# A fused audio tower on one core: the order of steps rewritten in two halves of two chunks, with top-2 per half

## Chip, core and metric

The kernel runs on one core of a Trainium2 chip. Its engines work side by side and each in its own program order: TensorE (PE, with its weight loads PEld), VectorE (DVE), ScalarE (ACT), GpSimd (POOL) and SyncE (SP), which here only issues DMAs. They wait for one another by semaphores. The metric is the device time of one execution in microseconds (us), lower is better; the median of the runs is compared.

## The reference

The input is 64 sequences of 375 steps with 16 features. Everything is float32. Five blocks follow one another, each but the first a residual on the layer norm of what is there:

```python
y = jnp.einsum('bpi,di->bpd', patches, W) + b          # 45 patches per sequence, D = 64
...
scores = jnp.einsum('bhqd,bhkd->bhqk', q, k) / jnp.sqrt(jnp.float32(HD)).astype(q.dtype)
attn = jax.nn.softmax(scores.astype(jnp.float32), axis=-1).astype(q.dtype)
...
probs = jax.nn.softmax(logits, axis=-1)
top2_vals, top2_idx = jax.lax.top_k(probs, 2)          # over 8 experts
h = jax.nn.gelu(xf @ w1 + bb1, approximate=False)      # every expert for every token
y = h @ w2 + bb2
...
S = S * dec_t[:, None, :] + sa[:, :, None] * b_t[:, None, :] + v_t[:, :, None] * k_t[:, None, :]
o_t = jnp.einsum('bvk,bk->bv', S, r_t)                 # a scan over the 45 tokens
...
ye = h @ Wr[l, e].T + br[l, e]                         # 2 layers, one of 16 experts per sequence
h = jax.nn.relu(shared + routed + h)
```

The kernel does the scan in closed form: it builds small triangular matrices per sequence, inverts them in levels, and multiplies.

## The kernel before

The 64 sequences are 32 pairs (two sequences lie on the two halves of the 128 partitions), and the pairs are `C` = 4 chunks of `PP` = 8 pairs. A chunk's activations are a tile of 128 x 360 floats (`W` = 8 x 45). All state of a chunk lies in its part of `arena`, and each chunk owns two of the eight PSUM banks (`PS`), so chunks are independent of each other; only the weights and the top-2 step are shared. Within a chunk nearly every step waits for the step ahead of it, because it uses the same two banks.

`schedule()` (L82) writes one list of steps `(name, i, c)`: a name, an index within it and a chunk. Each engine's program is made by walking that list and emitting its part of each step, so the list is the program order of all five engines. In the old list a stage runs over all four chunks before the next one starts; TensorE has three other chunks to work on while one waits for VectorE or ScalarE. The stages, by the names in the code:

- `tok`, two norms (`mean`, `var`), `q`, `k`, `v`: up to 49 us. They are the same after the change.
- attention: for each of 8 pairs and each chunk the scores `s` (TensorE, then maximum L611 and subtraction L613 on VectorE), exponential `e` (ScalarE L394), transposes `t` (TensorE L849, copy on ScalarE L397), weighted sum `pv` (TensorE, then reciprocal L621 and multiply L623 on VectorE). `LAG` = 2 is the distance between `t` and `pv` in units.
- `attT`, `wo`, norm 2, `gate`, then `top2`: one chain of 17 dependent steps on VectorE (L655 to L672) over all chunks' gate logits, with one exponential on ScalarE (L405), and a copy per chunk (L677). Then `cwT`, `cw2`, `b2` (the expert weights transposed and split in three bf16 parts).
- 8 experts: `hid` (TensorE, gelu on ScalarE L415) and `y` (TensorE, copy on ScalarE L419, multiply on VectorE L694, addition on GpSimd L313). `hid` of the next expert waits for the multiply of this one in the same chunk.
- norm 3 with `mixes`: its `var` step carries on VectorE the norm's product (L571), the difference of neighbours (L584, L585) and four mixes (L588); then `rk`, `vw`.
- the projections `aw`, `ab`, `gh`, `gg`, `kk`, `bon`, `kb`; `m`, `vt` and the inverse `lx`, `lt` in four levels; the solve `u`, `y2`, `z`, `w`, `o`; norm `gn`, `ro`, norm 5, `f`.
- the routed layers `r` (two layers, each 64 small matmuls of 32 columns per chunk against weights that SyncE gathered by DMA), `fo` and the output DMA.

ScalarE holds one set of function tables at a time. `tables(name)` (L350) emits a table load where the next function needs another set than the one loaded: exponential and logarithm are in one set, gelu and sigmoid/tanh each in another. SyncE's list: constants and input, 64 weight DMAs for routed layer 0, then 64 for layer 1, of which a chunk's 16 wait for that chunk's `h1` (attention added).

## Time and profile before

| | us |
|---|---|
| median of 3 runs | 394.02 |
| lowest, highest | 389.51, 397.53 |
| the profiled execution | 395.19 |
| its span on the core | 393.2 |
| TensorE busy in it | 326.8 (83%) |
| VectorE, ScalarE, GpSimd busy | 220.6, 197.7, 142.3 |

The profile is of one execution. The busy time of an engine is the sum of its instructions; what is left of the span it waits or has nothing to do. A matmul in float32 shows as two records, each with its weight load. The granted clock (PEclk) is given as a share of TensorE's full 2.4 GHz; the other level is 0.50, 1.2 GHz.

### The profile page before, as it was taken

What the parts mean: (1) busy time and instruction counts of PE and PEld (TensorE: products, weight loads), DVE (VectorE), ACT (ScalarE), POOL (GpSimd) and SP (SyncE); (2) the same over time, 40 slices, a digit from 0 to 9 for tenths busy, and PEclk for the clock granted to TensorE, in tenths of its full rate; (3) what the DMA queues carried; (4) which work ended last, traced back from release to release, by engine and by line L of the source; (5) the groups of instructions that cost most, each with busy time, mean ns of one, the idle gap of its engine ahead of it and who ended that gap; (6) DMA issues with size and microseconds to landing.
All of it is one profiled execution on the core that took longest, in us unless ns stands there. A gap on an engine that the chain in (4) does not pass through costs nothing.

```text
span 393.2 us, 13416 instructions
## 1 busy us (share of the span) xinstructions
PE 326.8 (83%) x5712; PEld 222.4 (57%) x5712; DVE 220.6 (56%) x446; ACT 197.7 (50%) x382; POOL 142.3 (36%) x146
## 2 busy tenths in 40 slices
PE   4999999999995999999677984597777799798465
PEld 2447876766862734343233544597776699345342
DVE  4567687787368632333595889965665303751002
ACT  1665465445454367677747794356000774646120
POOL 9009999512000055564243006699900000310000
PEclk9999999999997799999959998699999999879996
DMA  8622222110012221221000000000000000000002
GB/s 274 262 59 62 65 58 65 51 49 3 3 47 61 58 58 56 60 63 33 1 0 0 2 0 0 3 4 3 3 6 5 3 5 3 0 0 5 3 5 77
DMA packets 20563, 14.92 MB, mean 38 GB/s; under 512 B 2328, under 2 KB 19352, under 8 KB 20376
## 3 DMA queue, kind: packets, MB, share of 16 engines
q1 hardware_dynamic: 20504, 14.07, 11.5%
q8 instruction: 45, 0.74, 0.7%
q14 instruction: 14, 0.11, 0.1%
HBM read 13.32 MB, written 0.74 MB: 36 GB/s over the span
## 4 chain that ended last, share of the span: by engine, by line
PE 52%; DVE 17%; issue 12%; ACT 10%; POOL 8%; POOLq 0%; DVEq 0%
PE PS L785 48%; POOL arena L313 7%; PE PS L849 4%; DVE arena L588 2%; DVE arena L732 2%; DVE arena L571 2%; ACT arena L373 2%; ACT arena L370 1%; ACT arena L476 1%; ACT arena L485 1%; DVE PS L520 1%; ACT arena L489 1%; ACT arena L365 1%; DVE arena L735 1%; DVE arena L584 1%
## 5 line engine op out<-in xcount | busy, mean ns | idle before, releaser
L785 PE MATMUL PS<-arena,K 128*128 128x360 f32 (+2 forms) x576 | 149.7, 515 | 21.2 <-DVE arena L588 7.3
L785 PE MATMUL PS<-arena 128*45 128x45 f32 (+6 forms) x3648 | 118.5, 221 | 31.7 <-issue 15.4
L785 PEld LDWEIGHTS PS<-arena 128*45 128x45 f32 (+4 forms) x3648 | 100.7, 127 | 50.6 <-issue 36.4
L785 PEld LDWEIGHTS PS<-arena,K 128*128 128x128 f32 (+2 forms) x576 | 71.0, 183 | 81.8 <-issue 22.6
L313 POOL TENSOR_TENSOR arena<-arena 128x360 f32<-128x360 f32 x32 | 30.0, 948 | 68.8 <-DVE arena L694 68.2
L694 DVE TENSOR_TENSOR arena<-PS,arena 128x360 f32<-128x360 f32 x32 | 17.0, 533 | 33.7 <-ACT arena L419 33.7
L785 PE MATMUL PS<-K,arena 128*45 128x32 f32 (+4 forms) x768 | 26.1, 223 | 4.8 <-DVE arena L677 4.2
L785 PEld LDWEIGHTS PS<-K,arena 128*45 128x45 f32 (+2 forms) x768 | 25.3, 132 | 6.9 <-DVE arena L677 4.9
L397 ACT COPY arena<-PS 128x360 f32<-128x360 f32 x32 | 14.8, 467 | 24.5 <-PE PS L849 24.4
L415 ACT ACTIVATE arena<-PS,K 128x720 f32<-128x720 f32 x32 | 24.9, 861 | 2.5 <-PE PS L785 2.5
L341 POOL TENSOR_TENSOR arena<-arena 128x360 f32<-128x360 f32 x4 | 4.4, 1112 | 56.4 <-DVE arena L579 56.4
L302 POOL TENSOR_TENSOR arena<-arena,K 128x360 f32<-128x360 f32 x32 | 24.1, 799 | 0.0
L419 ACT COPY arena<-PS 128x360 f32<-128x360 f32 x32 | 14.8, 462 | 14.8 <-PE PS L785 14.8
L485 ACT ACTIVATE arena<-arena,K 128x360 f32<-128x360 f32 x8 | 4.3, 591 | 35.5 <-DVE arena L767 35.5
L849 PE MATMUL PS<-K,arena 128*128 128x128 f32 x128 | 20.8, 285 | 0.7 <-DVE arena L623 0.7
L571 DVE TENSOR_TENSOR arena<-arena 128x360 f32<-128x360 f32 x24 | 12.7, 531 | 14.8 <-ACT arena L373 14.8
L611 DVE TENSOR_REDUCE smax<-PS 128x8 f32<-128x360 f32 x32 | 16.9, 529 | 7.1 <-PE PS L785 7.0
L778 DVE SCALAR_TENSOR_TENSOR arena<-PS,K,arena 128x360 f32<-128x360 f32 x4 | 2.4, 593 | 32.5 <-PE PS L785 32.5
L365 ACT ACTIVATE arena<-arena 128x360 f32<-128x360 f32 x24 | 11.8, 503 | 17.1 <-DVE arena L565 15.7
L290 POOL TENSOR_TENSOR WG<-WG,K 128x2048 f32<-128x2048 f32 x4 | 15.2, 3816 | 13.2 <-DMA WG<-wr 13.2
L565 DVE TENSOR_TENSOR arena<-arena,PS 128x360 f32<-128x360 f32 x24 | 12.3, 528 | 10.4 <-PE PS L785 9.3
L394 ACT ACTIVATE arena<-arena 128x360 f32<-128x360 f32 x32 | 16.4, 513 | 3.3 <-DVE arena L613 3.3
(126 smaller groups left out, 420.2 us busy)
## 6 DMA issues: line engine op xcount, KB each, us to landing
WG<-wr SPq DMA_DIRECT2D x64, 64.0 KB, 1.9
arena<-wr SPq DMA_DIRECT2D x64, 64.0 KB, 1.8
arena<-xT SPq DMA_DIRECT2D x4, 368.0 KB, 4.8
K<-consts SPq DMA_DIRECT2D x1, 1171.0 KB, 10.7
K<-consts SPq DMA_DIRECT2D x1, 852.0 KB, 10.4
out<-arena SPq DMA_DIRECT2D x4, 180.0 KB, 1.9
K<-consts SPq DMA_DIRECT2D x1, 510.0 KB, 8.3
K<-consts SPq DMA_DIRECT2D x1, 352.0 KB, 9.1
```

Of the source, the lines that this page charges most:

```text
L290: g.tensor_tensor(w, w, shared, ALU.add).then_inc(sem["wsum"], 1)
L302: g.tensor_tensor(a(c, KX_ + i * W).rearrange("q (h t) -> q h t", t=T), a(c, slot(4) + i * T, T).unsqueeze(1).broadcast_to([128, NH, T]), ...
L313: g.tensor_tensor(a(c, H_), a(c, H_), a(c, slot(3 + i % 2)), ALU.add).then_inc(sem["acc"], 1)
L365: s.activation(a(c, sq), a(c, xc), ACT.Square).then_inc(sem["ln_sq"], 1)
L394: s.activation(pb, pb, ACT.Exp).then_inc(sem["s_exp"], 1)
L397: s.copy(a(c, PT_, 512).rearrange("q (r t) -> q r t", t=64)[:, :, 0:T], bank(c, 1, 512).rearrange("q (r t) -> q r t", t=64)[:, :, 0:T]).th ...
L415: s.activation(halves(a(c, slot(6), 2 * W)), both(c), ACT.Gelu, bias=k("b1", i, i + 1)).then_inc(sem["gelu"], 1)
L571: v.tensor_tensor(a(c, dst), a(c, xc), a(c, sq), ALU.mult).then_inc(sem["ln_out"], 1)
L611: v.tensor_reduce(smax[:, c, :], sc, AX.X, ALU.max).then_inc(sem["s_max"], 1)
L694: v.tensor_tensor(a(c, slot(3 + i % 2)), bank(c, 0), a(c, slot(8)), ALU.mult).then_inc(sem["y_mul"], 1)
L785: return nc.tensor.matmul(o, l, r, start=start, stop=stop)
L849: last = nc.tensor.transpose(bank(c, 1, 128, 128 * g), a(c, PB_ + 128 * g, 128), k("identf"))
```

## The change

The four chunks become two halves, a (chunks 0 and 1) and b (2 and 3). Up to the first scores everything stays. From attention on the new `schedule()` writes each block for one half, and `ahead(x, y)` merges two of them: it takes x step by step and puts in steps of y evenly between. So the list becomes: attention of a alone; attention of b with the after-attention steps of a; experts of a with the after-attention steps of b; experts of b with the mixes of a; mixes of b with projections of a; inverse of a with projections of b; inverse of b with solve and finish of a; solve of b alone; finish of b with the routed layers of a; routed layers of b. A step that is given as a list (norm 2's and norm 3's `var`, the first `hid`) is put in for both chunks of the half together. In attention the distance from `t` to `pv` is one unit where it was two. Top-2 runs once per half, over half of the elements, with its semaphore counts offset; the bias splitting moves from unit (4, 0) to (2, 0). Waits that counted steps in the old order now name chunk or step. No instruction of TensorE, GpSimd or SyncE is added or removed; VectorE has top-2's chain twice at half the size (the copies per chunk stay four in all), and ScalarE has 18 table loads where it had 5, and one exponential more.

```diff
+TOP2_STEPS = 17
...
+    halves_of_chunks = [range(0, C // 2), range(C // 2, C)]
+    def stage(cs, *steps):
+        return [(name, i, c) for name, i in steps for c in cs]
+    def norm(cs, k):
+        return stage(cs, ("mean", k), ("var", k))
+    def ahead(x, y):
+        out, taken = [], 0
+        for n, step in enumerate(x):
+            out.append(step)
+            while taken < len(y) and (taken + 1) * len(x) <= (n + 1) * len(y):
+                group = y[taken]
+                out += group if isinstance(group, list) else [group]
+                taken += 1
+        return out
+    def attention(cs):
+        out = []
+        units = [(i, c) for i in range(PP) for c in cs]
+        for n in range(len(units) + 1):
+            if n < len(units):
+                i, c = units[n]
+                out.append(("t", i, c))
+            if n:
+                out.append(("pv",) + units[n - 1])
+            if n < len(units) and i < PP - 1:
+                out.append(("s", i + 1, c))
+            if n:
+                i, c = units[n - 1]
+                if i < PP - 1:
+                    out.append(("e", i + 1, c))
+        return out
+    def after_attention(cs):
+        return (stage(cs, ("attT", 0), ("wo", 0)) + stage(cs, ("mean", 2)) + [stage(cs, ("var", 2))]
+                + stage(cs, ("gate", 0)) + [("top2", 0, cs[0])]
+                + [stage(cs, ("hid", 0))] + stage(cs, ("cwT", 0), ("cw2", 0), ("b2", 0)))
+    def experts(cs):
+        out = stage(cs, ("y", 0))
+        for i in range(1, E):
+            out += stage(cs, ("hid", i), ("y", i))
+        return out
+    def mix(cs):
+        out = stage(cs, ("mean", 3)) + [stage(cs, ("var", 3))]
+        for c in cs:
+            out += [("mixes", 0, c), ("rk", 0, c)]
+        return out + stage(cs, ("vw", 0))
+    def project(cs):
+        return stage(cs, ("aw", 0), ("ab", 0), ("gh", 0), ("gg", 0), ("kk", 0), ("bon", 0), ("kb", 0))
+    def invert(cs):
+        out = stage(cs, ("m", 0), ("m", 1), ("vt", 0))
+        for i in range(len(LEVELS)):
+            out += stage(cs, ("lx", i), ("lt", i))
+        return out
+    def solve(cs):
+        return stage(cs, ("u", 0), ("y2", 0), ("z", 0), ("w", 0), ("o", 0))
+    def finish(cs):
+        return norm(cs, 4) + stage(cs, ("ro", 0)) + norm(cs, 5) + stage(cs, ("f", 0))
+    def routed(cs):
+        return stage(cs, ("r", 0), ("r", 1), ("fo", 0))
+    a, b = halves_of_chunks
+    both_halves = range(C)
+    order = stage(both_halves, ("tok", 0)) + norm(both_halves, 0) + norm(both_halves, 1)
+    order += stage(both_halves, ("q", 0), ("k", 0), ("v", 0), ("s", 0), ("e", 0))
+    order += attention(a)
+    order += ahead(attention(b), after_attention(a))
+    order += ahead(experts(a), after_attention(b))
+    order += ahead(experts(b), mix(a))
+    order += ahead(mix(b), project(a))
+    order += ahead(invert(a), project(b))
+    order += ahead(invert(b), solve(a) + finish(a))
+    order += solve(b)
+    order += ahead(finish(b), routed(a))
+    order += routed(b)
+    flat = []
+    for step in order:
+        flat += step if isinstance(step, list) else [step]
+    return flat
...
-        def gate(r, n=C * PP * E):
-
-            return a(0, slot(14) + C * PP * E * r, n)
+        def gate(c, r, n=C // 2 * PP * E):
+
+            return a(c, slot(14) + C // 2 * PP * E * r, n)
...
                 elif name == "top2":
                     tables(LN_EXP)
                     act.wait_ge(sem["g_sub"], n)
-                    s.activation(gate(0), gate(0), ACT.Exp).then_inc(sem["g_exp"], 1)
+                    s.activation(gate(c, 0), gate(c, 0), ACT.Exp).then_inc(sem["g_exp"], 1)
...
-                    if (i, c) == (PP // 2, 0):
+                    if (i, c) == (2, 0):
                         split_biases()
...
                 elif name == "top2":
                     dve.wait_ge(sem["cst2"], 16)
-                    dve.wait_ge(sem["gate_mm"], C)
-                    steps = [0]
+                    dve.wait_ge(sem["gate_mm"], c + C // 2)
+                    steps = [TOP2_STEPS * (n - 1)]
+                    rows_here = C // 2 * PP
...
-                    step(v.tensor_tensor(chunks(gate(0)), logits,
-                                         k("gb").unsqueeze(1).unsqueeze(1).broadcast_to([128, C, PP, E]), ALU.add))
+                    step(v.tensor_tensor(chunks(gate(c, 0)), logits,
+                                         k("gb").unsqueeze(1).unsqueeze(1).broadcast_to([128, C // 2, PP, E]), ALU.add))
                     step(v.tensor_reduce(top, prob, AX.X, ALU.max))
                     v.tensor_tensor(prob, prob, wide(top), ALU.subtract).then_inc(sem["g_sub"], 1)
-                    dve.wait_ge(sem["g_exp"], 1)
+                    dve.wait_ge(sem["g_exp"], n)
...
-                    for cc in range(C):
+                    for cc in range(C // 2):
                         def thrice(r):
-                            return gate(r)[:, cc * small:(cc + 1) * small].rearrange(
+                            return gate(c, r)[:, cc * small:(cc + 1) * small].rearrange(
                                 "q (p e) -> q p e", e=E).unsqueeze(2).broadcast_to([128, PP, 3, E])
-                        v.tensor_tensor(a(cc, CW_, 3 * small).rearrange("q (p r e) -> q p r e", r=3, e=E), thrice(1),
+                        v.tensor_tensor(a(c + cc, CW_, 3 * small).rearrange("q (p r e) -> q p r e", r=3, e=E), thrice(1),
                                         thrice(0), ALU.mult).then_inc(sem["cw"], 1)
...
                 elif name == "hid":
                     if i == 0:
-                        pe.wait_ge(sem["g_steps"], 1)
+                        pe.wait_ge(sem["g_steps"], TOP2_STEPS * (c // (C // 2)) + 1)
                     else:
                         pe.wait_ge(sem["y_mul"], COUNT["y", i - 1, c])
...
                 elif name == "y":
                     if i == 0:
-                        pe.wait_ge(sem["cwT"], n)
-                        pe.wait_ge(sem["b2_add"], n)
-                    pe.wait_ge(sem["gelu"], n)
+                        pe.wait_ge(sem["cwT"], c + 1)
+                        pe.wait_ge(sem["b2_add"], c + 1)
+                    pe.wait_ge(sem["gelu"], COUNT["hid", i, c])
```

How the lists of instructions move, at three places. Rows are instructions in program order, with a count where several alike follow; the line numbers of the new kernel are 37 or 38 higher.

VectorE, around the first top-2 (its chain begins at L655 before, at L693 now). Before, all of attention is done, and the norm of four chunks stands ahead of it:

```order
L621 RECIPROCAL orec<-PS 128x8
L623 TENSOR_TENSOR arena<-PS,orec 128x64
L629 TENSOR_TENSOR arena<-arena,PS 128x360 x4
L565 TENSOR_TENSOR arena<-arena,PS 128x360 x4
L571 TENSOR_TENSOR arena<-arena 128x360 x4
L655 TENSOR_TENSOR arena<-PS,K 128x256
L657 TENSOR_REDUCE arena<-arena 128x32
L658 TENSOR_TENSOR arena<-arena 128x256
L660 TENSOR_REDUCE arena<-arena 128x32
L661 RECIPROCAL arena<-arena 128x32
```

After: softmax and weighted sum of the second half's attention (L648, L650, L658, L660) stand ahead of and behind it.

```order
L648 TENSOR_REDUCE smax<-PS 128x8
L650 TENSOR_TENSOR arena<-PS,smax 128x8x45
L658 RECIPROCAL orec<-PS 128x8
L660 TENSOR_TENSOR arena<-PS,orec 128x64
L693 TENSOR_TENSOR arena<-PS,K 128x128
L695 TENSOR_REDUCE arena<-arena 128x16
...
L706 TENSOR_TENSOR arena<-arena 128x128
L710 TENSOR_TENSOR arena<-arena 128x128
L715 TENSOR_TENSOR arena<-arena 128x192 x2
L648 TENSOR_REDUCE smax<-PS 128x8
L650 TENSOR_TENSOR arena<-PS,smax 128x8x45
L658 RECIPROCAL orec<-PS 128x8
```

The chain has moved from a place between two stages to the middle of attention, and acts on 128 elements where it acted on 256.

VectorE, in the experts and the mixes behind them (L694, now L732, is an expert's multiply; L588, now L625, the mixes). Before:

```order
L689 TENSOR_TENSOR arena<-arena,PS 128x360 x4
L694 TENSOR_TENSOR arena<-PS,arena 128x360 x32
L565 TENSOR_TENSOR arena<-arena,PS 128x360 x4
L571 TENSOR_TENSOR arena<-arena 128x360
L584 TENSOR_TENSOR arena<-arena 128x8x44
L585 TENSOR_SCALAR arena<-arena 128x8
L588 SCALAR_TENSOR_TENSOR arena<-arena,K 128x360 x4
L571 TENSOR_TENSOR arena<-arena 128x360
L584 TENSOR_TENSOR arena<-arena 128x8x44
```

After, in the second half's experts:

```order
L602 TENSOR_TENSOR arena<-arena,PS 128x360
L732 TENSOR_TENSOR arena<-PS,arena 128x360 x2
L608 TENSOR_TENSOR arena<-arena 128x360
L621 TENSOR_TENSOR arena<-arena 128x8x44
L622 TENSOR_SCALAR arena<-arena 128x8
L625 SCALAR_TENSOR_TENSOR arena<-arena,K 128x360 x4
L608 TENSOR_TENSOR arena<-arena 128x360
L621 TENSOR_TENSOR arena<-arena 128x8x44
L622 TENSOR_SCALAR arena<-arena 128x8
L625 SCALAR_TENSOR_TENSOR arena<-arena,K 128x360 x4
L732 TENSOR_TENSOR arena<-PS,arena 128x360 x3
L738 TENSOR_SCALAR arena<-arena,K 128x360
```

The first half's mixes now stand between two multiplies of the second half's experts.

TensorE, towards the end (32x45 are the small matmuls of the routed layers, 128x360 x2 from two arena tiles the steps of the last norms). Before, the last norms and the first layer:

```order
L785 MATMUL PS<-arena 64x45 x128
L785 MATMUL PS<-arena,K 128x360 x28
L785 MATMUL PS<-oneh,rb_split 128x360 x2
L785 MATMUL PS<-arena,WG 32x45 x64
L785 MATMUL PS<-oneh,rb_split 128x360 x2
L785 MATMUL PS<-arena,WG 32x45 x64
```

After, from the second half's first mean on:

```order
L823 MATMUL PS<-arena,K 128x360 x2
L823 MATMUL PS<-oneh,rb_split 128x360 x2
L823 MATMUL PS<-arena,WG 32x45 x64
L823 MATMUL PS<-arena,K 128x360 x2
L823 MATMUL PS<-oneh,rb_split 128x360 x2
L823 MATMUL PS<-arena,WG 32x45 x64
L823 MATMUL PS<-arena,K 128x360 x2
L823 MATMUL PS<-oneh,rb_split 128x360 x2
L823 MATMUL PS<-arena 32x45 x64
L823 MATMUL PS<-arena,K 128x360 x2
L823 MATMUL PS<-oneh,rb_split 128x360 x2
L823 MATMUL PS<-arena 32x45 x64
```

Norm steps of the second half now stand between the routed passes of the first, where eight passes followed one another.

## Rows read from the trace of the kernel before

**Rows 1.** The page, busy time, share and instructions of each engine.

```profile
PE 326.8 (83%) x5712; PEld 222.4 (57%) x5712; DVE 220.6 (56%) x446; ACT 197.7 (50%) x382; POOL 142.3 (36%) x146
```

**Rows 2.** Windows: start:end, length, each engine's busy time (instructions), PEclk, DMA.

```profile
49.00:102.20 53.20, 52.50 (x676) 36.92 (x675) 42.57 (x122) 27.01 (x62) 28.54 (x23) 1.00 0.15 42
102.20:136.50 34.30, 28.11 (x482) 21.09 (x481) 21.10 (x50) 16.33 (x31) 0.00 (x0) 0.85 0.16 47
136.50:189.60 53.10, 52.95 (x279) 20.65 (x279) 19.29 (x38) 36.33 (x62) 29.98 (x32) 1.00 0.18 51
189.60:215.00 25.40, 15.87 (x39) 7.98 (x39) 17.61 (x34) 16.98 (x32) 6.95 (x7) 0.80 0.00 0
215.00:252.10 37.10, 26.60 (x220) 18.04 (x220) 33.01 (x52) 22.98 (x45) 13.17 (x14) 0.92 0.00 1
252.10:303.90 51.80, 41.08 (x1594) 39.92 (x1596) 31.53 (x43) 13.88 (x30) 30.50 (x29) 0.96 0.02 4
303.90:333.80 29.90, 26.36 (x960) 25.96 (x954) 8.98 (x15) 18.98 (x35) 0.00 (x0) 1.00 0.02 4
333.80:356.40 22.60, 19.18 (x57) 9.55 (x56) 14.24 (x24) 13.07 (x27) 4.45 (x4) 0.85 0.00 1
356.40:386.00 29.60, 17.70 (x1046) 13.56 (x1044) 0.00 (x0) 7.44 (x11) 0.00 (x0) 0.94 0.01 4
...
386.00:393.20 7.20, 4.25 (x16) 1.48 (x16) 2.37 (x4) 0.75 (x1) 0.00 (x0) 0.74 0.28 105
```

**Rows 3.** Timeline in attention: start, length, engine, line, what [idle before].

```profile
59.58 0.53 DVE L611 TENSOR_REDUCE smax<-PS 128x8 f32<-128x360 f32 x1 [0.33 <-PE PS L785]
...
60.97 0.51 ACT L394 ACTIVATE arena<-arena 128x360 f32<-128x360 f32 x1
...
61.37 0.53 DVE L611 TENSOR_REDUCE smax<-PS 128x8 f32<-128x360 f32 x1 [0.32 <-PE PS L785]
```

**Rows 4.** Instructions grouped by line and shape: busy us, mean ns, idle.

```profile
L694 DVE TENSOR_TENSOR arena<-PS,arena 128x360 f32<-128x360 f32 x32 | 17.0, 533 | 33.7 <-ACT arena L419 33.7
...
L419 ACT COPY arena<-PS 128x360 f32<-128x360 f32 x32 | 14.8, 462 | 14.8 <-PE PS L785 14.8
...
L550 DVE SCALAR_TENSOR_TENSOR K<-rb_split,K 51x256 f32<-51x256 bf16 x1 | 0.5, 476 | 0.0
```

**Rows 5.** Timeline in top-2: VectorE's first and last rows, ScalarE's switch.

```profile
118.79 0.43 DVE L655 TENSOR_TENSOR arena<-PS,K 128x256 f32<-128x256 f32 x1 [1.02 <-PE PS L785]
...
127.40 1.16 DVE L677 TENSOR_TENSOR arena<-arena 128x192 f32<-128x192 f32 x4
...
120.59 1.28 ACT L352 ACT_TABLE_LOAD   x1
121.89 3.11 ACT L415 ACTIVATE arena<-PS,K 128x720 f32<-128x720 f32 x4
```

**Rows 6.** Timeline of TensorE in the first experts.

```profile
138.53 0.83 PE L785 MATMUL PS<-arena,K 128*64 128x360 f32 x4
...
139.55 0.83 PE L785 MATMUL PS<-arena,K 128*64 128x360 f32 x4
...
140.56 3.45 PE L785 MATMUL PS<-arena,K 64*128 64x360 f32 x20
```

**Rows 7.** Timeline of VectorE in norm 3, one chunk's start to the next.

```profile
197.21 0.53 DVE L571 TENSOR_TENSOR arena<-arena 128x360 f32<-128x360 f32 x1
...
201.83 0.52 DVE L571 TENSOR_TENSOR arena<-arena 128x360 f32<-128x360 f32 x1
```

**Rows 8.** Timeline of TensorE in the first routed layer.

```profile
362.60 1.35 PE L785 MATMUL PS<-arena,WG 128*32 128x45 f32 x111
365.99 0.39 PE L785 MATMUL PS<-arena,WG 128*32 128x45 f32 x17 [2.04 <-issue]
```

**Rows 9.** Windows around top-2, columns as in group 2.

```profile
124.00:126.00 2.00, 0.00 (x0) 0.00 (x0) 1.85 (x5) 1.00 (x2) 0.00 (x0) 1.00 0.22 66
128.00:130.00 2.00, 2.00 (x60) 2.00 (x58) 0.81 (x4) 0.46 (x1) 0.00 (x0) 0.50 0.22 64
```

64 lines of the change are left out of this document (8 added, 56 removed).

## The prediction

> **What bounds the kernel now.** I read the busy times first: TensorE is busy for 326.8 of 393.2 us, so all that an order can win is its idle 66 us [rows 1]. Next the busy times by stage, to see where that idle time lies [rows 2]. In attention and in the eight experts TensorE is full: 52.50 of 53.20 us and 52.95 of 53.10. The holes are elsewhere: 6.2 us between attention and experts (34.30 less 28.11), 9.5 in the token mixes, 10.5 in the projections, 10.7 in the triangular inverse, 3.5 in the solve, 3.4 in norms and output projection, 14.9 in the routed layers with the tail (17.70 busy of 29.60, then 4.25 of 7.20). They have three causes. First, one engine works while TensorE waits: top-2 holds VectorE from 118.79 to 128.56 [rows 5]; in the projections VectorE is busy 33.01 of 37.10 us [rows 2]. Second, TensorE runs 111 short matmuls in 1.35 us and then nothing until 365.99, which the trace puts down to issue, not to a wait [rows 8]. Third, the clock: in 124 to 126 TensorE did nothing, and in 128 to 130 it runs at 0.50 of full speed, the lower level of 1.2 GHz [rows 9].
>
> **The parts, costed.** The 66 us can be filled only where two halves overlap, and each half now has two chunks in flight instead of four. I went through the new order engine by engine: a step starts when its engine has done the step ahead of it and its inputs are there. The first 49 us don't change. Each stretch below is set against half of the old stages in it [rows 2].
>
> (1) Attention of the first half, alone. The old pace is one unit per 1.79 us (59.58 to 61.37). From the end of a score matmul, two VectorE operations (0.53 each) and the exponential (0.51) must end before that chunk's transposes, some 1.7 us with hand-overs [rows 3]. The new order puts transposes, weighted sum and scores of the other chunk in between, 1.8 us of TensorE. So it just fits, and 16 units take 28.8. The four bias-splitting operations, at most 0.48 each [rows 4], now lie in a loop without slack, +1.5. Total 30.5, against 26.6: **+3.9**.
>
> (2) Attention of the second half with the after-attention steps of the first. TensorE has 26.3 us of attention and half of 28.11 at mean clock 0.85, 12: 38.3. The second top-2 cost is new: top-2 took 9.8 us for four chunks (118.79 to 128.56) [rows 5]. With half the elements its 17 steps save only some 0.13 us each (an estimate: 0.42 at 256 elements and 0.53 at 360 make 1 ns per element) and two of four copies go, so 7.0 us remain, per half; bounds are 9.3 (no operation gets shorter) and 4.9 (everything halves), 2 us either way in (2) and in (3). Behind it in VectorE's queue stands the softmax of the next unit; TensorE has 3.8 us left that needs none of it and idles some 5.4. The grouped variance steps hold ScalarE for four operations, 2 us more. Rest 1: 46.7 against 26.6 + 17.2 = 43.8: **+2.9**.
>
> (3) Experts of the first half with the after-attention steps of the second. An output takes 1.01 us of TensorE (138.53 to 139.55), a hidden layer (3.45 - 0.83) / 4 = 0.65 [rows 6]; four of each make the 6.64 us that an expert takes now. With four chunks the chain hidden, gelu (0.78), output, copy (0.46), multiply (0.53) [rows 4 to 6] hides behind the other three; with two it takes some 3.75 us against 3.3 us of matmuls, which the inserted steps fill. 16 outputs and 14 hidden layers are 25.3 us; 25.3 + 12 = 37.3, and 4.5 of stalls, mostly top-2 again with two table loads at 1.28 [rows 5]: 41.8 against 43.8: **-2.0**.
>
> (4) Experts of the second half with the mixes of the first. TensorE: 25.3 and half of 15.87 at clock 0.80, with its last matmuls some 7: 32.3. But the variance group carries all mixing: 4.6 us per chunk on VectorE (197.21 to 201.83) [rows 7], two chunks in a row, behind a table load, a logarithm and an exponential. The experts' next multiply waits behind that; TensorE has one round, 3.3 us, to run meanwhile: 8 us lost. Four more table loads sit between two gelus or behind them, 4 us. Total 44.3 against 26.6 + 12.7 = 39.3: **+5.0**.
>
> (5) Mixes of the second half with projections of the first: VectorE has (17.61 + 33.01) / 2 = 25.3 us [rows 2]; with waits for table loads 29, against 31.3: **-2.3**. (6) Inverse of the first half with projections of the second: VectorE again, (31.53 + 33.01) / 2 = 32.3 plus the last level's 3, and 6 of waits, since a chunk's 4 us of scaling steps stand ahead of the inverse's subtractions: 41.6 against 18.5 + 25.9 = 44.4: **-2.8**. (7) Inverse of the second half with solve and norms of the first: TensorE (41.08 x 0.96 + 26.36 + 19.18 x 0.85) / 2 = 41, start stall 4.5, rest 1: 46.7 against 25.9 + 15.0 + 11.3 = 52.2: **-5.5**. (8) Solve of the second half alone: 15.1 against 15.0: **0**. (9) Norms of the second half with the routed layers of the first: the routed layers' issue gaps (11.9 us idle in eight passes) and the norms' waits cover each other: 19 against 11.3 + 14.8 = 26.1: **-7.1**. (10) Routed layers of the second half and the tail: 20.6 against 14.8 + 7.2 = 22.0, the tail having two outputs to write instead of four: **-1.4**. No DMA moves into the way: the 64 layer-1 weight loads start when a chunk's attention has been added, earlier for the first half, and are needed only in (6).
>
> Sum: +3.9 + 2.9 - 2.0 + 5.0 - 2.3 - 2.8 - 5.5 - 7.1 - 1.4 = -9.3, with all matmuls behind the new holes at full clock. They won't be: five holes of 3 us and more (one in 2, one in 3, two in 4, one at the start of 7, one in 8) can each be followed by some 5 us at 0.50, as in [rows 9], which costs 2.5 where TensorE is what is waited for: 0 to 13 us, less what before loses so and after wins back. I take +6, the middle. That is -3.3 on the profiled execution of 395.2: 391.9. The median of the runs is 394.0, which would make 390.7. **391 us.**
>
> A page speaks against the change. The new order needs 18 table loads where the old has 5. In the trace a load takes 1.28 us and the gelu starts at 121.89, 0.02 after it [rows 5], so the 13 added loads cost at most 16.7 us. The Trainium skill (ScalarE: Activation LUTs, What ACT_TABLE_LOAD costs) says that each switch takes 1283 ns and about 1380 ns of drain on top. By that rule the 13 loads would cost 34.6 us, and the sum, which exposes about a third of them, would be some 6 us higher; the trace agrees with the first figure and shows no drain.
>
> **The rivals.** *The holes fill* (0.30): ScalarE and VectorE waits overlap better than my walk has it, the clock stays up. For it: 66 us idle against the 9 that I win. Then the -9.3 stands, or twice that: 376 to 386. *Table loads decide* (0.12; slower): every added load lands between a matmul and the gelu, tanh or logarithm that TensorE waits for, in (3) to (5). Against it: many are issued while ScalarE waits anyway. By the page's rule above this rival would cost 17.9 us more; the trace is against that part. My sum has about 6 of the 16.7 exposed; all make +11: 402. It ends slower once more than about 11 of the 13 are exposed. *Attention does not fit* (0.11; slower): the slack of 0.1 us per unit in (1) isn't there. Each of 32 units longer by 0.35 gives +11, 402. It decides from 0.33 us per unit. Against it: the steps in [rows 3] add up to just under the pace. *The order does nothing* (in my case): gains at the end equal losses in the middle, 395.
>
> **How the numbers follow.** My forecast has 0.47: 384 to 399. A measurement of this kernel tells about 2% from no change, 386 to 402. Faster: nearly all of the first rival and the low edge of mine, 0.34. Slower: most of the two slow rivals and a little of mine, 0.20. Within 2%: 0.46. The range leaves out the best fifth of the fast rival and the worst of the slow ones: 377 to 404.
>
> **What would show it.** Attention of the first half at 1.8 us per unit, ending near 80 us. Two top-2 blocks of about 7 us on VectorE, each with a TensorE hole of 3 to 5. A hole of about 8 us in TensorE within the second half's experts. The routed layers of the first half without issue gaps of 1.5 to 2 us. TensorE's mean clock below 0.94. I'm wrong if attention runs at over 2 us per unit, if the table loads follow straight on waits of TensorE throughout, or if the span to the start of the second half's routed layers is far from 369 (the stretches up to there, with the clock's 6).

## The result and the profile after

The changed kernel takes 427.65 us, the median of 4 runs (424.81 to 429.6); the kernel before, measured beside it, 393.91 us (389.51 to 397.53). The ratio is 1.089, with a 95% interval of 1.077 to 1.101: slower by 9%, outside the predicted range of 377 to 404. The profiled execution has a span of 422.7 us and a mean granted clock of 0.922; the kernel before had 393.2 us and 0.943.

The page of the changed kernel, busy times, answers to [rows 1]:

```profile
PE 343.2 (81%) x5712; PEld 220.7 (52%) x5712; DVE 242.5 (57%) x464; ACT 218.5 (52%) x396; POOL 143.1 (34%) x146
```

TensorE has the same 5712 matmuls. Its idle time has grown from 66.4 to 79.5 us and its busy time from 326.8 to 343.2. Two questions: where is the new idle time, and how can the same matmuls be busy for longer?

The busy times by window, cut where the prediction's ten stretches begin and end, answer to [rows 2] (columns as there):

```profile
49.00:94.00 45.00, 28.62 (x356) 19.01 (x354) 35.89 (x64) 15.20 (x32) 27.70 (x22) 0.81 0.18 51
94.00:144.50 50.50, 43.14 (x588) 28.93 (x586) 32.65 (x94) 23.34 (x47) 0.00 (x0) 0.93 0.15 44
144.50:188.20 43.70, 39.33 (x354) 16.96 (x356) 20.07 (x48) 32.02 (x50) 14.40 (x15) 1.00 0.16 45
188.20:236.80 48.60, 40.21 (x163) 14.98 (x163) 17.43 (x36) 33.70 (x53) 19.62 (x21) 0.90 0.02 5
236.80:269.20 32.40, 21.10 (x97) 11.52 (x97) 25.85 (x43) 23.39 (x41) 9.32 (x10) 0.87 0.00 1
269.20:318.20 49.00, 39.36 (x1009) 32.04 (x1007) 38.94 (x52) 21.97 (x43) 21.96 (x21) 0.88 0.01 3
318.20:368.20 50.00, 47.41 (x1398) 39.86 (x1394) 29.40 (x43) 22.88 (x46) 18.38 (x17) 0.99 0.01 4
368.20:383.20 15.00, 12.06 (x323) 11.47 (x324) 2.26 (x4) 7.65 (x14) 0.00 (x0) 0.89 0.01 2
383.20:403.20 20.00, 16.14 (x547) 9.39 (x545) 7.00 (x13) 9.18 (x17) 2.11 (x2) 1.00 0.02 4
403.20:422.70 19.50, 13.59 (x536) 8.93 (x536) 2.26 (x4) 4.79 (x6) 0.00 (x0) 0.80 0.12 41
```

The first stretch stands out: 45.0 us, of which TensorE works 28.62, while VectorE is "busy" 35.89. What TensorE waited for, over the whole kernel (total us, times, longest), puts it in one row, the first:

```profile
PE PS L887 <- ACT arena L431: 21.4, 5, 14.1
...
PE PS L823 <- issue: 5.2, 6, 1.6
```

The transposes (L887) waited 14.1 us in one piece for an exponential (L431), which waited for VectorE's subtraction. VectorE's timeline there, and GpSimd's:

```profile
59.35 9.87 DVE L585 CAST rb_split<-K 51x256 bf16<-51x256 f32 x1
69.25 0.48 DVE L587 SCALAR_TENSOR_TENSOR K<-rb_split,K 51x256 f32<-51x256 bf16 x1
69.76 3.79 DVE L590 CAST rb_split<-K 51x256 bf16<-51x256 f32 x1
73.58 0.48 DVE L592 SCALAR_TENSOR_TENSOR rb_split<-rb_split,K 51x256 bf16<-51x256 bf16 x1
...
55.49 5.31 POOL L339 TENSOR_TENSOR arena<-arena,K 128x360 f32<-128x360 f32 x7
60.76 0.78 POOL L318 TENSOR_TENSOR K<-K 128x128 f32<-128x128 f32 x2
61.49 7.58 POOL L327 TENSOR_TENSOR WG<-WG,K 128x2048 f32<-128x2048 f32 x2
69.58 3.82 POOL L327 TENSOR_TENSOR WG<-WG,K 128x2048 f32<-128x2048 f32 x1 [0.51 <-DMA WG<-wr]
```

These are the four operations of the bias splitting, which the change moved from unit (4, 0) to unit (2, 0). A cast of 51x256 elements takes 9.87 us, and the second 3.79. In the kernel before, the same two took 0.28 and 0.29 us, at 82.55:

```profile
82.55 0.28 DVE L548 CAST rb_split<-K 51x256 bf16<-51x256 f32 x1
...
83.37 0.29 DVE L553 CAST rb_split<-K 51x256 bf16<-51x256 f32 x1
...
62.37 11.36 POOL L290 TENSOR_TENSOR WG<-WG,K 128x2048 f32<-128x2048 f32 x3
86.88 3.81 POOL L290 TENSOR_TENSOR WG<-WG,K 128x2048 f32<-128x2048 f32 x1 [13.15 <-DMA WG<-wr]
```

The long casts end when GpSimd stops: the first at 69.22, in the 0.51 us in which GpSimd waits for a DMA (61.49 + 7.58 = 69.07 to 69.58), the second at 73.55, behind the last addition (73.40). Each ends about 0.15 us behind that. In the old order the splitting fell into GpSimd's wait of 13.15 us. That is a reading so far; the experiments test it.

### The profile page after: what moved, and what is told of

Same layout as the page of the kernel before. It is cut to its first block, busy times and chain, and to the rows that moved or that the text cites. A ratio compares the mean times of both kernels' runs of the same rounds, so it can differ in the third digit from the quotient of the medians.

```text
span 422.7 us, 13449 instructions
## 1 busy us (share of the span) xinstructions
PE 343.2 (81%) x5712; PEld 220.7 (52%) x5712; DVE 242.5 (57%) x464; ACT 218.5 (52%) x396; POOL 143.1 (34%) x146
## 4 chain that ended last, share of the span: by engine, by line
PE 52%; DVE 23%; ACT 16%; issue 5%; POOL 2%; POOLq 0%; DVEq 0%
PE PS L823 49%; PE PS L887 3%; DVE rb_split L585 2%; ACT L389 2%; DVE arena L625 2%; ACT arena L407 2%; DVE arena L608 2%; ACT arena L410 2%; DVE arena L650 1%; ACT arena L452 1%; DVE smax L648 1%; DVE arena L732 1%; ACT arena L513 1%; ACT arena L402 1%; ACT arena L456 1%
## 5 line engine op out<-in xcount | busy, mean ns | idle before, releaser
L823 PE MATMUL PS<-arena,K 128*128 128x360 f32 (+2 forms) x576 | 157.4, 515 | 27.8 <-ACT arena L452 7.8
L823 PE MATMUL PS<-arena 128*45 128x45 f32 (+6 forms) x3648 | 131.2, 227 | 23.7 <-ACT arena L502 10.8
L823 PEld LDWEIGHTS PS<-arena 128*45 128x45 f32 (+4 forms) x3648 | 108.3, 132 | 46.0 <-issue 36.0
L823 PEld LDWEIGHTS PS<-arena,K 128*128 128x128 f32 (+2 forms) x576 | 64.7, 178 | 84.3 <-issue 22.0
L887 PE MATMUL PS<-K,arena 128*128 128x128 f32 x128 | 21.5, 293 | 22.0 <-ACT arena L431 21.4
L732 DVE TENSOR_TENSOR arena<-PS,arena 128x360 f32<-128x360 f32 x32 | 16.8, 532 | 36.5 <-ACT arena L456 36.5
L887 PEld LDWEIGHTS PS<-K,arena 128*128 128x128 f32 x128 | 14.8, 147 | 34.9 <-ACT arena L431 32.3
L452 ACT ACTIVATE arena<-PS,K 128x720 f32<-128x720 f32 x32 | 26.6, 860 | 7.2 <-PE PS L823 7.1
L823 PEld LDWEIGHTS PS<-K,arena 128*45 128x45 f32 (+2 forms) x768 | 24.4, 125 | 7.5 <-issue 4.2
L431 ACT ACTIVATE arena<-arena 128x360 f32<-128x360 f32 x32 | 16.4, 514 | 19.2 <-DVE arena L650 19.0
L648 DVE TENSOR_REDUCE smax<-PS 128x8 f32<-128x360 f32 x32 | 16.9, 529 | 12.9 <-PE PS L823 12.9
L456 ACT COPY arena<-PS 128x360 f32<-128x360 f32 x32 | 14.5, 460 | 14.4 <-PE PS L823 14.1
L327 POOL TENSOR_TENSOR WG<-WG,K 128x2048 f32<-128x2048 f32 x4 | 15.2, 3813 | 14.5 <-DMA WG<-wr 14.5
```

Source lines behind the costliest of these rows:

```text
L431: s.activation(pb, pb, ACT.Exp).then_inc(sem["s_exp"], 1)
L452: s.activation(halves(a(c, slot(6), 2 * W)), both(c), ACT.Gelu, bias=k("b1", i, i + 1)).then_inc(sem["gelu"], 1)
L456: s.copy(a(c, slot(8)), bank(c, 1)).then_inc(sem["cwb"], 1)
L648: v.tensor_reduce(smax[:, c, :], sc, AX.X, ALU.max).then_inc(sem["s_max"], 1)
L732: v.tensor_tensor(a(c, slot(3 + i % 2)), bank(c, 0), a(c, slot(8)), ALU.mult).then_inc(sem["y_mul"], 1)
L823: return nc.tensor.matmul(o, l, r, start=start, stop=stop)
```

## The experiments

Theory P: the casts wait for GpSimd, and that is the main cause. Rival Q: the new attention loop (two chunks, a distance of one unit) is slow by itself. Behind that comes what is left over. All ratios are to the kernel before, measured on the same chip in the same session. The runs fall into four sessions on different chips, in which the kernel before took 389.9 to 395.4 us, so two runs of different sessions are compared by their ratios and not by their times.

**1. The splitting at another place in the changed kernel.**

```diff
-                    if (i, c) == (2, 0):
+                    if (i, c) == (6, 1):
                         split_biases()
```

> The changed kernel with one edit: the bias splitting moves from unit (2, 0) of attention to unit (6, 1), at about 76 us, where GpSimd has ended its layer-0 additions and waits for a DMA until 87 us. Theory P (the two casts of the splitting, 9.87 and 3.79 us in the changed kernel's trace where they took 0.28 in the old one, wait for GpSimd's additions of weights, which run at 61.5 to 73.4 us): each cast is back at about 0.3 us, TensorE's hole of 14.13 us at 75.7 goes but for 1 to 1.5 us, and the kernel takes 12.5 to 14 us less than the changed one, so a ratio to the kernel before of 1.053 to 1.057. Rival Q (the new attention loop with a distance of one unit is what is slow, and the casts only show a wait that the loop has anyway): the hole moves to the new place or is spread over the units, and the time stays within 3 us of the changed kernel, ratio 1.08 to 1.09.

407.48 us against 395.41; ratio 1.026 (1.017 to 1.036), where 1.053 to 1.057 was expected. The profile (span 405.8) has both casts at their usual length, and the first stretch takes 29.8 us instead of 45.0:

```profile
L590 DVE CAST rb_split<-K 51x256 bf16<-51x256 f32 x1 | 0.3, 285 | 0.0
L585 DVE CAST rb_split<-K 51x256 bf16<-51x256 f32 x1 | 0.3, 275 | 0.0
```

```profile
49.00:78.80 29.80, 27.37 (x360) 18.11 (x357) 23.54 (x66) 15.71 (x33) 24.65 (x22) 1.00 0.22 61
```

P holds and Q falls: the loop itself costs 29.8 us, near what was forecast. The gain is larger than expected: 15.2 us in this stretch and 16.9 between the spans (by the ratios it is more, 1.089 to 1.026). It is the hole, and a granted clock of 1.00 in this stretch where it was 0.81. Some 10 to 12 us of the loss remain.

**2. The splitting early in the kernel before.**

```diff
-                    if (i, c) == (PP // 2, 0):
+                    if (i, c) == (2, 0):
                         split_biases()
```

> The kernel before with one edit: the bias splitting moves from unit (4, 0) to unit (2, 0), at about 63 us, where GpSimd adds its layer-0 weights (62.4 to 73 us in the old trace). Theory P: the casts take together 8 to 12 us as in the changed kernel, and with four chunks in turn on TensorE the hole behind them is 7 to 12 us: ratio 1.02 to 1.03. Rival Q (the order of the halves is the cause): ratio 1.00, both casts about 0.3 us. Between them lies: the casts are long but the other chunks hide most of it, ratio 1.01.

400.67 us, 5.3 more than before, ratio 1.010 (1.002 to 1.019): little as a time, but the trace is plain. One move of four short operations, nothing else, and a hole appears in a stage that had none:

```profile
68.33 5.76 DVE L548 CAST rb_split<-K 51x256 bf16<-51x256 f32 x1
...
62.55 11.38 POOL L290 TENSOR_TENSOR WG<-WG,K 128x2048 f32<-128x2048 f32 x3
```

```profile
PE PS L849 <- DVE arena L623: 6.0, 1, 6.0
```

The first cast ends at 74.09, 0.15 us behind the last of three additions (73.94), and the second, with GpSimd idle, takes 0.28. The hole is below the expected 7 to 12 us because here, with four chunks in turn, a unit comes round more slowly: unit (2, 0) comes at 68.33, 9 us later, so less of GpSimd's work is left to wait for.

**3. The splitting in place, GpSimd's additions later.**

```diff
             def shared_plus_identity():
 
+                pool.wait_ge(sem["h1"], 2)
                 pool.wait_ge(sem["cst4"], 16)
```

> The changed kernel with the bias splitting left at unit (2, 0), but GpSimd begins its layer-0 additions of weights only when attention has been added in chunks 0 and 1 (about 95 us in this kernel). Theory P: the casts take about 0.3 us each, the hole at 75.7 goes, and 12 to 14 us come back, less what the additions cost at their new place: they then run beside norm 2 and the first top-2, whose VectorE operations read two tiles of SBUF, so up to one addition (3.8 us) may be lost there again. Ratio 1.055 to 1.07. Rival Q: ratio 1.08 to 1.09 and long casts or a hole at the same place with GpSimd idle.

418.69 us, ratio 1.060 (1.052 to 1.068), within the expected 1.055 to 1.07: better than the changed kernel (1.089), and 11.2 us slower than run 1 in the same session. The first cast takes 1.58 us (GpSimd still runs its last products of attention), the second 0.28. The rest went where the expectation feared. The additions now run from 94.84 to 110.53 without a gap, and the norm's product (L609, two inputs in SBUF, 0.53 us as a rule) is caught in two chunks:

```profile
94.84 15.70 POOL L328 TENSOR_TENSOR WG<-WG,K 128x2048 f32<-128x2048 f32 x4
...
102.37 4.10 POOL L328 TENSOR_TENSOR WG<-WG,K 128x2048 f32<-128x2048 f32 x1
...
101.44 1.36 DVE L609 TENSOR_TENSOR arena<-arena 128x360 f32<-128x360 f32 x1 [0.63 <-ACT arena L411]
102.72 4.14 DVE L609 TENSOR_TENSOR arena<-arena 128x360 f32<-128x360 f32 x1
106.79 0.19 DVE L659 RECIPROCAL orec<-PS 128x8 f32<-128x8 f32 x1
```

These two products behave otherwise than the casts. The first addition that they meet ends at 102.41, the next at 106.47, and each product ends 0.39 us behind one of these, though the following addition has begun by then: a product waits for one addition and gets in ahead of the next. The addition that it gets ahead of is the one that pays, 4.10 us for 3.81. The cast of the changed kernel passed five such places, between operations of GpSimd that followed each other, and got in at none of them.

The operations on PSUM behind it (L659 and on) run at their usual length while the additions go on to 110.53.

**4. Another instruction in place of the cast.**

```diff
-                v.tensor_copy(hi, rb).then_inc(sem["rb_steps"], 1)
+                v.tensor_tensor(hi, rb, rb, ALU.max).then_inc(sem["rb_steps"], 1)
```

> The changed kernel with the splitting at its place, but the two casts (one input in SBUF) are written as a maximum of the tile with itself (two inputs in SBUF, bfloat16 out, the same values). Theory P1 (it is the cast as such that waits for GpSimd: only it is held among VectorE's operations): the maximum takes about 0.5 us, and 12.5 to 14 us come back, ratio 1.053 to 1.057. Theory P2 (a VectorE operation with two inputs in SBUF waits too, as the product L752 of 0.53 us that takes 4.03 us at 288.5 us beside the layer-1 additions would have it): the maximum takes 9 to 10 and 3 to 4 us as the casts do, ratio 1.08 to 1.09. The Trainium skill (SBUF — State Buffer, Who interferes with whom) is on P2's side: by it both forms contend with a GpSimd operation that reads SBUF.

The four runs took 421.01 to 431.88 us against 395.41, that is 1.065 to 1.092 of it, too wide a spread to choose between P1 (1.053 to 1.057) and P2 (1.08 to 1.09) by a ratio. The trace chooses. P2 holds in kind: this operation, which is no cast and has its two inputs in SBUF, is caught too. Its size is another than expected, one wait of 13.76 us in place of one of 9 to 10 and one of 3 to 4. It waits for everything that GpSimd has in a row, products, sums and three additions, from 60.36 to 74.12; the second maximum (74.66, 0.42 us) then meets nothing:

```profile
60.36 13.76 DVE L585 TENSOR_TENSOR rb_split<-K 51x256 bf16<-51x256 f32 x1
...
49.72 12.08 POOL L339 TENSOR_TENSOR arena<-arena,K 128x360 f32<-128x360 f32 x16
61.76 0.78 POOL L318 TENSOR_TENSOR K<-K 128x128 f32<-128x128 f32 x2
62.49 11.34 POOL L327 TENSOR_TENSOR WG<-WG,K 128x2048 f32<-128x2048 f32 x3
```

The rule stands in the Trainium skill (SBUF — State Buffer, Who interferes with whom): VectorE and GpSimd share one pair of ports as an exclusive lock, which a VectorE operation needs when it has two inputs in SBUF or is a cast or copy in a two-port mode. The runs agree on what is caught (9.87, 5.76 and 13.76 us, and 0.28 or 0.42 with GpSimd idle). The same section has the lock held for the whole instruction; how long a VectorE operation waits when GpSimd's instructions follow each other differs between the runs here, from the rest of one addition (run 3) to all that are in a row (this run).

**5. The other place with the same pattern.** In the changed kernel, and in run 1, GpSimd's layer-1 additions meet the projections of the second half. Of run 1, where L749 waits for the first addition (to 272.30), L752 for the second (to 276.17):

```profile
271.27 1.23 DVE L749 TENSOR_SCALAR arena<-arena,K,oneka 128x360 f32<-128x360 f32 x1
272.54 4.03 DVE L752 TENSOR_TENSOR arena<-arena 128x360 f32<-128x360 f32 x1
...
268.49 7.68 POOL L327 TENSOR_TENSOR arena<-arena,K 128x2048 f32<-128x2048 f32 x2
```

The edit, on top of run 1's:

```diff
-                elif name == "lx" and i == 0:
-                    add_shared(1, c)
+                elif name == "lx" and i < 2 and c >= C // 2:
+                    add_shared(1, 2 * i + c - C // 2)
```

> The order in halves with the splitting moved to unit (6, 1), and beside it GpSimd's four layer-1 additions of weights (3.85 us each) moved from the inverse of each half (a's lay beside the projections of b, at 268.5 to 276.2 us in that kernel) to the first two levels of the inverse of b. Theory P (a VectorE operation with both inputs in SBUF waits for GpSimd's addition: L752 took 4.03 us where it takes 0.53, L749 1.23 for 0.46, and TensorE had a hole of 2.6 us behind L802): these operations are back at their usual length and 3 to 5 us go against the kernel with the splitting alone moved, ratio 1.013 to 1.02. Rival Q (the hole is given back by the next wait, since VectorE and ScalarE bound this stretch): 0 to 1.5 us go, ratio 1.022 to 1.03.

404.03 us, ratio 1.029 (1.021 to 1.037), not to be told from run 1's 1.026: as a time it is the rival's 1.022 to 1.03. The mechanism is confirmed in its stretch: L752 takes 0.53 again, L749 0.46, and from the first eviction of `m` in chunk 0 to that in chunk 2 it is 44.4 us instead of 47.5. Whether those 3 us reach the end can't be resolved with these intervals. A third operation is caught in the changed kernel, in run 1 and still in this one (2.50 us here), the scaling L810 of the solve, which takes 0.49 us in the second half. Of the changed kernel:

```profile
336.01 2.49 DVE L810 TENSOR_SCALAR arena<-arena,K 128x512 f32<-128x512 f32 x1
```

**6. The table loads.** Every function that needs a set becomes sigmoid, and one load is made, in run 1's order and in the old one (in both outputs the functions are missing).

```diff
-                if loaded[0] != name:
-                    s.preload_act_table_set(name)
+                if loaded[0] is None:
+                    s.preload_act_table_set("sigmoid_and_others")
```

> The order in halves with the splitting moved (as in the run that moved it to unit (6, 1)), but every function of ScalarE that needs a set is replaced by sigmoid and one table load is made in all instead of 18: the output leaves out exponential, logarithm, gelu and tanh, the instructions and their sizes stay. To be read against the same edit of the kernel before. Theory T (the 13 added loads of 1.28 us, 16.7 us of ScalarE, are what the middle loses): the order in halves comes within 3 us of the kernel before under the same edit. Theory N (most loads fall in ScalarE's idle time or beside other holes, and the middle loses by its chains): it stays 8 to 12 us behind it, as with the loads (12.1 us between medians).

> The kernel before with every set function of ScalarE replaced by sigmoid and one table load instead of 5: the output leaves out exponential, logarithm, gelu and tanh. It is the control of the run with the halves. Four loads of 1.28 us go, of which the one in top-2 (120.59 us) and the one ahead of the first gelu lie on TensorE's path. Both theories: 1 to 5 us less than before, ratio 0.988 to 1.0.

402.40 us (1.025, 1.018 to 1.032) and 390.43 us (0.995, 0.992 to 0.998): 12.0 us apart, where run 1 and the kernel before are 12.1 apart with the loads. Theory N: 13 more loads cost the order in halves nothing that can be measured. The hole in experts b with mixes a shows it at one place: it was 3.49 us behind two loads, and stays 3.36 without them, now behind VectorE's norm and mixes for two chunks (6.5 us in a row).

**7. Top-2.** Run 1 with each half's chain cut from 17 to 9 waited steps (`TOP2_STEPS = 9`; the output leaves out the second expert).

> The order in halves with the splitting moved to unit (6, 1), and top-2's chain cut from 17 to 9 waited steps in each half (the output leaves out the second expert and the choice among equals): 8 steps of 0.325 us, 2.6 us a half. Theory S (the chain of each half lies on TensorE's path: it stands idle 3.06 us at 111.0 and 1.40 at 106.2 behind a's): 4 to 6 us less than with the splitting alone moved, half a stretch of lower clock behind it gone too, ratio 1.011 to 1.017. Rival U (only a's lies there, b's hides under the experts): 2 to 3 us less, ratio 1.018 to 1.022. Rival V (given back at the next wait): ratio 1.024 to 1.03.

405.22 us, ratio 1.036 (1.027 to 1.044): no gain to be seen, which is rival V's reading, though above its 1.024 to 1.03. TensorE's wait behind the first chain went only from 3.25 to 2.58 us.

**8. Only the end in halves.** The kernel before up to the inverse, then solve a; solve b with finish a; finish b with routed a; routed b.

```diff
+    order += solve(a)
+    order += ahead(solve(b), finish(a))
+    order += ahead(finish(b), routed(a))
+    order += routed(b)
```

> The kernel before, order unchanged through the inverse (four chunks a stage, top-2 once, bias splitting at unit (4, 0), 5 table loads); only its end is cut in halves, as the change does: solve of a, then solve of b with finish of a, finish of b with the routed layers of a, routed layers of b. The waits on the weights' sum name layer and chunk as in the change. Theory E (the change's end gains what the milestones of the changed kernel show, 6.1 us in finish b with routed a and 2.5 us in routed b with the tail, and its middle loses): 6 to 11 us less than before, ratio 0.972 to 0.985. Rival F (the end gains only because the middle left an idle ScalarE and VectorE behind, or the granted clock takes it back): ratio 0.99 to 1.005.

392.64 us, ratio 1.001 (0.996 to 1.005), over 10 and 17 runs: nothing.

**9. Halves from the inverse, and halves from norm 3.** The old order up to `kb` in the one, up to the last expert in the other, and the change's order behind.

```diff
+    order += invert(a)
+    order += ahead(invert(b), solve(a) + finish(a))
```

```diff
+    order += mix(a)
+    order += ahead(mix(b), project(a))
+    order += ahead(invert(a), project(b))
+    order += ahead(invert(b), solve(a) + finish(a))
```

> The kernel before, its order unchanged through the projections (kb); from there the halves as the change has them: inverse of a alone, inverse of b with solve and finish of a, solve of b, finish of b with the routed layers of a, routed layers of b. Theory G (the change's late stretches are good: between the first m of b and the end the order in halves took 102.3 us with the splitting moved, where half an inverse and the stages behind it take 109.5 us in the kernel before): 3 to 7 us less than before, less 1 to 3 us for the inverse of a alone with two chunks to turn over; ratio 0.98 to 0.995. Rival F (as with the solve and norms in halves, which gave nothing: what the merge hides comes back in matmul bursts that no longer follow each other and in the clock): ratio 0.995 to 1.01.

> The kernel before, its order unchanged through the experts; from norm 3 on the halves as the change has them, starting with the mixes of a alone. It splits what is left of the loss (12.1 us with the splitting moved) at the last expert. Theory M (the loss lies in the stretches ahead of it: attention b with after-attention a at 50.1 us for 43.8, experts a at 46.5 for 43.8, experts b with mixes a at 47.8 for 39.3, together 17.5 us; from mixes b on the same kernel took 181.9 us where the halves of before take 191 us): mixes of a alone take 13 to 17 us, and this kernel takes 5 us less to 2 us more than before, ratio 0.987 to 1.005. Rival R (it lies in the projections and the inverse merged with them, where TensorE waits 9.1 and 8.0 us): 6 us or more above before, ratio 1.015 or more.

From the inverse: 390.06 us against 392.42, ratio 0.994 (0.990 to 0.998), the only order tried here that beats both kernels, by 0.6%, a small gain whose interval leaves out 1. From norm 3: 392.11 us, ratio 1.001 (0.997 to 1.004), theory M. Its profile cuts the loss cleanly. Norm 3 of the second half begins (its square on ScalarE) at 206.80 in it and at 223.93 in run 1; from there to the end it is 182.0 us (span 388.8) in the one and 181.9 (405.8) in the other. So all that run 1 loses against this order, 17 us, lies ahead of that point: in attention, top-2 and the experts, with what is put in between them.

**10. The experts in halves, alone.**

```diff
+    for cs in (range(0, C // 2), range(C // 2, C)):
+        order += [("y", 0, c) for c in cs]
+        for i in range(1, E):
+            order += [("hid", i, c) for c in cs] + [("y", i, c) for c in cs]
```

> The kernel before with one edit: the experts of chunks 0 and 1 run first, then those of chunks 2 and 3, with nothing beside them; all else in the old order. Theory H (two chunks can't cover the round of hid, gelu, y, copy and multiply: two chunks have 3.34 us of TensorE work an expert, half of the 6.68 us pitch of four chunks, and a chunk's round takes about 4.6 us by its parts, 0.65 + 0.84 + 1.0 + 0.46 + 0.53 and four hand-overs of 0.2 to 0.3): TensorE waits about 1.3 us an expert, 16 times, so 15 to 22 us more than before, ratio 1.04 to 1.055. Then the experts in halves of the change live on their filling, and where the other half's steps leave a place empty or come in a bunch TensorE stands. Rival I (two chunks are enough, the round is covered): ratio 0.995 to 1.01.

400.81 us against 389.86, ratio 1.028 (1.019 to 1.036). Theory H has the sign, not the size: 11 us instead of 15 to 22. TensorE's timeline of one expert:

```profile
149.93 2.66 PE L787 MATMUL PS<-arena,K 64*128 64x360 f32 x12
152.52 0.33 PE L787 MATMUL PS<-arena,KB 128*128 128x360 bf16 x1
152.78 0.83 PE L787 MATMUL PS<-arena,K 128*64 128x360 f32 x4
153.54 0.33 PE L787 MATMUL PS<-arena,KB 128*128 128x360 bf16 x1
153.97 2.66 PE L787 MATMUL PS<-arena,K 64*128 64x360 f32 x12
```

One expert of two chunks takes 153.97 - 149.93 = 4.04 us; in the old order, with four, 6.68 (the copy L419 of chunk 0 stands at 151.16 and 157.84), so 3.34 for two. That is 0.70 us a pass, 10 us over 14 passes. Little of it shows as idle. The list of waits has none here, and the window of six passes, 24.23 us, has TensorE busy for 22.79:

```profile
140.77:165.00 24.23, 22.79 (x110) 7.15 (x112) 6.39 (x12) 15.85 (x24) 11.36 (x12) 1.00 0.21 61
```

So 0.24 us of a pass are idle, in gaps too short for the list, and 0.46 are counted as busy. 20 such records take 3.45 us in [rows 6], 12 take 2.66 here. The two hidden layers (8 records) should take 1.31 us and take 1.83, because the second waits for its multiply. Instruction by instruction, a record of a hidden layer lasts 0.46 us and the next pair starts 0.30 us behind it; where the second layer waits, its first pair starts 0.60 us behind (150.34 to 150.94), so that only the last 0.14 us are a gap, and that pair lasts 0.57. The rest of the wait stands as busy time.

**11. Loads and mixes together.** As the table loads alone gave nothing, three of VectorE's four mixes are left out as well, in both orders (`for u in (0,):` and `wait_ge(sem["xi"], n)`).

> The order in halves with the splitting moved and one table load in all (functions replaced by sigmoid), and beside it three of the four mixes that VectorE makes in a chunk behind norm 3 are left out (12 operations of 0.53 us in all; the output leaves out three mixes besides the functions). Its control is the same edit of the kernel before. Theory J (in experts b with mixes a the table loads of ScalarE and the mixes of VectorE cover each other, so that taking away the loads alone gave nothing: the hole of 3.49 us at 189.4 stayed as 3.36): the halves gain 5 to 8 us against the run without loads and come within 8 us of their control. Theory K (the loss of 12 us between the orders is spread over bursts that no longer follow each other and over the clock): both orders gain the same 2 to 4 us, and 10 to 13 us stay between them.

> The control: the kernel before with one table load in all and one mix of four on VectorE (the output leaves out the functions and three mixes). TensorE's wait of 4.6 us for the first chunk's mixes shortens by up to 3 times 0.53 us, and the later chunks' by as much where VectorE is what they wait for: 2 to 6 us less than the kernel before without loads, ratio 0.98 to 0.99, by both theories.

393.24 us (1.011, 1.005 to 1.016) and 383.43 us (0.983, 0.975 to 0.990), 9.8 us apart, by the ratios 11. Against their twins without loads the ratios fall from 1.025 to 1.011 and from 0.995 to 0.983, some 5.5 and 4.9 us: the control as expected, the halves at the lower edge of J, but the distance between the two orders stays as K has it. J explains at most 2 us of it. The two pages are worth a look side by side, halves first:

```profile
span 389.4 us, 13420 instructions
...
PE 334.0 (86%) x5712; PEld 215.9 (55%) x5712; DVE 223.5 (57%) x452; ACT 196.0 (50%) x379; POOL 142.9 (37%) x146
```

```profile
span 381.7 us, 13400 instructions
...
PE 324.2 (85%) x5712; PEld 223.0 (58%) x5712; DVE 214.8 (56%) x434; ACT 192.7 (50%) x378; POOL 142.1 (37%) x146
```

TensorE idles 55.4 us in the order in halves and 57.5 in the old one, at nearly the same clock (0.959, 0.955). The loss, 7.7 us between these two spans, is all in its busy time: 9.8 us more for the same 5712 matmuls. Run 1 against the kernel before shows the same (342.0 for 326.8 busy, 63.8 for 66.4 idle). Run 10 says what such busy time can be: short waits inside bursts that used to follow each other closely. That it is the same in the other stretches is not shown.

## Why the prediction was wrong, by its own steps

Stretch by stretch, in us. The predicted sum has 6 more for the clock; run 1 is the changed kernel with the splitting moved, its windows cut at the same steps.

| stretch | half of before | predicted | changed | run 1 |
|---|---|---|---|---|
| 1 attention a | 26.6 | 30.5 | 45.0 | 29.8 |
| 2 attention b, after-attention a | 43.8 | 46.7 | 50.5 | 49.8 |
| 3 experts a, after-attention b | 43.8 | 41.8 | 43.7 | 46.5 |
| 4 experts b, mixes a | 39.3 | 44.3 | 48.6 | 47.9 |
| 5 mixes b, projections a | 31.3 | 29 | 32.4 | 31.7 |
| 6 inverse a, projections b | 44.4 | 41.6 | 49.0 | 47.5 |
| 7 inverse b, solve and norms a | 52.2 | 46.7 | 50.0 | 49.2 |
| 8 solve b | 15.0 | 15.1 | 15.0 | 13.5 |
| 9 norms b, routed a | 26.1 | 19 | 20.0 | 19.6 |
| 10 routed b, tail | 22.0 | 20.6 | 19.5 | 21.3 |
| sum | 344.5 | 335.3 + 6 | 373.7 | 356.8 |

**The step that failed first: "The four bias-splitting operations, at most 0.48 each, now lie in a loop without slack, +1.5".** The term cost 15.2 us in its own stretch (45.0 against 29.8) and 16.9 between the spans of the changed kernel and run 1. I took the durations from [rows 4], measured at 82 us, when GpSimd was idle, and carried them to 59 us without asking what GpSimd does there; its additions from 62.37 to 73.7 stood in the same trace. Run 1 (moved away: gone), run 2 (moved there in the old kernel: a cast of 5.76 us and TensorE idle for 6.0), run 3 (additions moved: casts of 1.58 and 0.28, another operation caught) and run 4 (a maximum with two SBUF inputs is caught as well) settle it. The rest of the stretch was nearly right: without the splitting's wait it takes 29.8 us, for 28.8 predicted. The units alternate 1.75 and 1.96 us (52.40 and 54.15 in the rows below, then 56.11), 1.86 on average where [rows 3] have 1.79, which makes 29.7 for 16. So the rival in which attention doesn't fit was rightly held unlikely; it needed 0.33 us per unit.

```profile
52.40 0.53 DVE L648 TENSOR_REDUCE smax<-PS 128x8 f32<-128x360 f32 x1 [0.39 <-PE PS L823]
...
54.15 0.53 DVE L648 TENSOR_REDUCE smax<-PS 128x8 f32<-128x360 f32 x1 [0.28 <-PE PS L823]
```

**The step that failed second: stretches 2 to 6, put at +0.8 against halves of the old stages.** In run 1 they take 223.4 us for 202.6, +20.8. The large stalls were seen, and were not what was missing. Top-2 is as predicted, 7.0 us against 6.76 (122.65 to 129.41), with TensorE waiting 1.40 and 3.26 us:

```profile
122.65 0.28 DVE L693 TENSOR_TENSOR arena<-PS,K 128x128 f32<-128x128 f32 x1
...
128.78 0.63 DVE L715 TENSOR_TENSOR arena<-arena 128x192 f32<-128x192 f32 x2
```

The mixes of two chunks hold VectorE for 6.5 us and TensorE for 3.5, where I had put 9.2 and 8, and the table loads, put at 4 in stretch 4, cost nothing that run 6 could find. Stretch 4 still takes 47.9 us for 44.3, so its pace was put too low by more than the 3.6 that the table shows, some 8 to 12 (an estimate, with those two terms corrected). What failed is the method: each stretch was TensorE's matmuls at their old pace plus the waits above 2 us. In attention and experts the old order had TensorE full (52.50 of 53.20 and 52.95 of 53.10 us in [rows 2]), so nothing could be won there, and the pace itself was a product of four chunks in turn. With two, an expert costs 0.70 us more (run 10; I had 3.75 us a pass, it is 4.04, and I let the inserted steps fill the difference to 3.3 entirely). That the inserted steps of the other half fill some of that and bring waits of their own is my reading; no run took them apart. The same holds for stretch 6, where the subtractions of the inverse queue behind the scaling steps as foreseen, and the layer-1 additions catch L752, about 3 us that I had not seen (run 5). How the remaining 10 us or so divide among single waits stays open: no one thing that was taken away (loads, half of top-2, mixes, additions) gave more than a few us of them back.

**What was right.** Stretches 7 to 10: 101.4 predicted, 104.5 in the changed kernel, 103.6 in run 1, for 115.3. The routed layers' issue gaps fell from 20.4 us in 17 waits to 5.2 in 6, as forecast. But the same end behind the old middle won nothing (run 8), and with the inverse in halves 0.6% (run 9): the inverse of a alone, from the first eviction of `m` in chunk 0 to that in chunk 2, takes 31.3 us where half of the old one takes 25.9, which eats half of the 11.4 us that come back behind it. The rival in which table loads decide had 0.12 and is refuted (run 6). The clock was put at +6. In the changed kernel it stood lower, 0.911 to 0.924 in its four runs; with the splitting moved it did not, 0.937 to 0.957 in run 1 beside 0.926 to 0.944 for the kernel before, so the order by itself did not lower it. Two of the signs that were to show the forecast wrong came: attention of the first half takes 45.0 us for 16 units, 2.8 each, all through one hole, and the second half's routed layers begin at 403.2 us (in run 1 at 384.5) for 369. Two of the sums slip by 0.3 and 0.2 us (stretches 6 and 7 add up to 41.3 and 46.5), which changes nothing.

None of my rivals had a VectorE operation waiting for another engine without a semaphore, and my price for an operation that moves had an upper bound taken from the same undisturbed place. Had I bounded the casts by how long GpSimd works there, from 59 to 73.7 us, the sum would have been 14 us higher, 405, which has the sign right and is still 22 short: the rest is the second step.
